# Score blocks transposed in two half-row tiles per pair of heads, in a two-layer attention kernel on one Trainium2 core

## The reference

```python
x = x + L0_attn(layernorm(x))   # 16 heads of 8; logits = q k^T / sqrt(8) - alpha[h] |i - j|
x = x + tanh(((layernorm(x) @ weight) @ aux1) @ aux2 + bias)
x = x + L1_attn(layernorm(x))   # low-rank k and v; scores = (q k^T / sqrt(128)) * exp(-0.01 |i - j|)
x = x + L1_ffn(layernorm(x))    # +-1 weights 256x512, 512x512, 512x128; relu(..) * 2 between them
```

## Time and profile before

| | |
|---|---|
| median of three runs | 350.02 us |
| span of the profiled execution | 348.8 us |
| PE, PEld busy | 330.2 us, 244.0 us |
| DVE, ACT, POOL busy | 275.9, 271.7, 261.3 us |
| item of layer 0, steady state | 17.3 to 18.1 us |
| item of layer 1, steady state | 21.3 us |

### The profile page before, as it was taken

The page is one execution under the profiler, slowest core; times in us unless marked ns, Lnnn a source line. Parts: engine busy times, 40 slices in busy tenths (PEclk is TensorE's granted clock), DMA queues, the critical chain, the costliest instruction groups (busy, mean ns, idle before and its releaser), DMA issues.

```text
span 348.8 us, 11196 instructions
## 1 busy us (share of the span) xinstructions
PE 330.2 (95%) x3550; PEld 244.0 (70%) x3550; DVE 275.9 (79%) x1367; ACT 271.7 (78%) x586; POOL 261.3 (75%) x655
## 2 busy tenths in 40 slices
PE   6599979999999999999999999999999999999986
PEld 4276757777776777777666767777787777778675
DVE  6877778898988998989988888768777677668246
ACT  3576874877776777777878889989898898888943
POOL 7368665676767666767969899898998988898430
PEclk9969998999999999999999999999999999999999
DMA  5202532223233323232332223224132331111001
GB/s 141 69 1 70 161 118 77 97 78 111 84 105 92 95 85 103 78 110 83 105 96 93 80 88 105 74 76 127 36 108 63 89 115 41 43 34 48 2 17 30
DMA packets 42390, 28.14 MB, mean 81 GB/s; under 512 B 9111, under 2 KB 38494, under 8 KB 42334
## 3 DMA queue, kind: packets, MB, share of 16 engines
q1 hardware_dynamic: 41768, 27.18, 26.4%
q10 hardware_dynamic: 566, 0.26, 0.3%
HBM read 14.09 MB, written 13.09 MB: 78 GB/s over the span
## 4 chain that ended last, share of the span: by engine, by line
PE 74%; DVE 9%; DMA 5%; issue 4%; ACT 3%; POOL 2%; SPq 1%; POOLq 0%; DVEq 0%; ACTq 0%
PE bank L551 20%; PE bank L566 14%; PE bank L548 8%; PE bank L592 7%; PE bank L526 5%; PE bank L540 5%; PE bank L613 4%; PE bank L605 3%; DVE scored L854 3%; DMA den_rows<-dden 3%; PE bank L574 2%; PE bank L658 1%; DMA dacc<-acc_sb 1%; PE bank L758 1%; POOL scored L1332 1%
## 5 line engine op out<-in xcount | busy, mean ns | idle before, releaser
L1093 ACT ACTIVATE probs<-bank 128x512 f32<-128x512 f32 x256 | 147.9, 599 | 47.6 <-PE bank L551 31.7
L854 DVE CUSTOM_DVE_ANT_0 scored<-bank,decay 128x256 f32<-128x256 f32 x256 | 93.1, 417 | 28.4 <-PE bank L526 28.2
L551 PE MATMUL bank<-ident,scored 128*128 128x128 f32 x736 | 108.6, 279 | 2.2 <-ACT probs L1093 1.4
L1332 POOL TENSOR_SCALAR scored<-scored,negbias 128x256 f32<-128x256 f32 x224 | 105.5, 487 | 3.1
L854 DVE CUSTOM_DVE_ANT_0 scored<-bank,adist 128x256 f32<-128x256 f32 x256 | 93.1, 417 | 11.0 <-PE bank L526 7.8
L551 PEld LDWEIGHTS bank<-ident,scored 128*128 128x128 f32 x736 | 81.8, 142 | 27.1 <-issue 19.4
L566 PE MATMUL bank<-probs,vpad 128*32 128x256 f32 x1024 | 69.2, 388 | 0.0
L1323 POOL TENSOR_SCALAR negbias<-mx 128x2 f32<-128x2 f32 x144 | 32.8, 237 | 32.0 <-DVE mx L854 31.1
L548 PE MATMUL bank<-ident,scored 128*128 128x128 f32 x288 | 44.4, 278 | 0.0
L566 PEld LDWEIGHTS bank<-probs,vpad 128*32 128x32 f32 x1024 | 26.9, 109 | 24.9 <-ACT probs L1093 7.2
L854 DVE DVE_READ_ACCUMULATOR2_ANT mx<- 128x1 f32 x512 | 42.1, 82 | 0.0
(11 more groups left out here) (196 smaller groups left out, 442.7 us busy)
## 6 DMA issues: line engine op xcount, KB each, us to landing
dqk<-parts SPq DMA_DIRECT2D x120, 64.0 KB, 2.0
stack<-dqk SPq DMA_DIRECT2D x30, 256.0 KB, 2.8
dacc<-acc_sb SPq DMA_DIRECT2D x15, 256.0 KB, 2.2
att_rows<-dacc SPq DMA_DIRECT2D x15, 128.0 KB, 2.6
den_rows<-dden SPq DMA_DIRECT2D x15, 128.0 KB, 2.5
out_dram<-outb SPq DMA_DIRECT2D x7, 128.0 KB, 1.8
x_sb<-in_L_attn_x_dram SPq DMA_DIRECT2D x1, 640.0 KB, 4.7
den_in<-acc_sb SPq DMA_DIRECT2D x30, 8.0 KB
```

The costliest lines, as they stand in the source:

```text
L551: mm = pe.transpose(dst, src, ident[:, :])
L854: red = dve.tensor_tensor_reduce(scored[:, r, t, :], bank[c % QUAD][:, t * T:(t + 1) * T], tab[:, (1 - t) * P:(1 - t) * P + T], 1.0, NEG_B ...
L1093: act.activation(probs[:, c % RING, :, :], turn_bank(c)[:, :].rearrange("p (a c) -> p a c", a=2), ACT.Exp).then_inc(probs_ready, 1)
L1332: sh = pool.tensor_scalar(scored[:, r, t, :], scored[:, r, t, :], negbias[:, 2 * r + t:2 * r + t + 1], 1.0, ALU.add, ALU.mult)
```

## The change

- Heads are turned in pairs. `pe_turn` takes heads 2n and 2n + 1 together. It splits the 128 query rows into two halves of 64. The upper half uses rows 0 to 63 of the array, the lower half rows 64 to 127, each with its own bank. A transpose of 128 x 128 becomes two of 64 rows: the loaded operand is 64 x 128, the streamed one (the identity) has 64 columns. A pair has 16 such transposes, 8 per tile, where it had 8 of full size.
- The two banks of a pair hold each a half of the rows of both heads. `act_exp` reads them one after the other, and the next pair may start only when the banks it takes are read. Both heads and both halves are released by one semaphore at the end of the turn. The banks are 4 and 5, but in layer 0 pair 6 of 8 takes 4 and 6, so pair 7, which takes 5 and 4, waits only for the first exponential of pair 6.
- P is now a property of a pair. `SHIFT` gives 8 of 16 heads to P in layer 0 (7 before) and 6 of 16 in layer 1 (2 before). A P pair has 8 extra products, 4 per tile, of 64 rows and 128 columns. A heads: 3 and 2 (1 and 3 before); G: 4 and 5 (5 and 9 before); D: 1 and 3 (3 and 2 before).
- The heads of D, A and G are written as maximum minus score, and the exponential takes the scale -1. This drops the 144 `negbias` instructions on POOL: the shift reads `mx` itself.
- The product with v stands one slot later (`PV_LAG` 10), banks 6 and 7 change places, all slots are set anew, and the loads of the ±1 weights are issued over items 1 to 3 and not all in item 0.

```diff
+SCORE_AT = 1
+TURNS = (((4, 5), (4, 5), (4, 5), (4, 5), (4, 5), (5, 4), (4, 6), (5, 4)),
+         ((4, 5), (5, 4), (4, 5), (4, 5), (5, 4), (5, 4), (5, 4), (4, 5)))
...
-SHIFT = ("PPGP" "DGGD" "GDPP" "PPGA", "GGGD" "GGAP" "PGDG" "AGAG")
+SHIFT = ("PPAD" "PPPP" "GGPP" "GAGA", "GDDG" "PPGG" "PPDG" "PPAA")
...
-    def pe_turn(pe, c):
-
...
-        need(pe, probs_ready, c + 1 - len(TURN_BANKS))
-        out, r = turn_bank(c), c % RING
-        for t in range(QT if kind == "P" else 0):
-            pe.matmul(out[:, :].rearrange("p (k t q) -> p t k q", k=QT, t=QT)[:, t, :, :],
-                      negmax[:, 2 * r + t:2 * r + t + 1].to_broadcast([P, P]),
-                      ident16[:, :].unsqueeze(1).to_broadcast([P, QT, P]), start=(t == 0), stop=False,
-                      skip_group_check=True)
-        for k in range(QT):
-            for t in range(QT):
-                src, dst = scored[:, r, t, k * P:(k + 1) * P], out[:, k * T + t * P:k * T + (t + 1) * P]
-                if kind == "P":
-                    mm = pe.matmul(dst, src, ident[:, :], start=False, stop=True, is_transpose=True,
-                                   skip_group_check=True)
-                else:
-                    mm = pe.transpose(dst, src, ident[:, :])
+    def pe_turn(pe, n):
+
+
+        pair = (2 * n, 2 * n + 1)
+        banks = turn_banks(n)
+        if pair_is_p(n):
+            pe.wait_ge(shift_p, shifts_p(n + 1))
+        else:
+            for c in pair:
+                kind = shift_of(c)
+                pe.wait_ge({"D": shift_d, "A": shift_a, "G": shift_g}[kind], shifts(kind, c + 1))
+        for b in banks:
+            bank_free(pe, b)
+        halves = [(bank[b], HALF_ROWS * h, slice(HALF_ROWS * h, HALF_ROWS * h + HALF_ROWS))
+                  for h, b in enumerate(banks)]
+
+        for e, t in [(e, t) for e in range(2) for t in range(QT)] if pair_is_p(n) else ():
+            col = 2 * ((2 * n + e) % RING) + t
+            for out, row, rows in halves:
+                pe.matmul(out[:, e * T:e * T + T].rearrange("p (k t q) -> p t k q", k=QT, t=QT)[:, t, :, :],
+                          negmax[rows, col:col + 1].to_broadcast([HALF_ROWS, P]),
+                          ident16[rows, rows].unsqueeze(1).to_broadcast([HALF_ROWS, QT, HALF_ROWS]),
+                          start=(e == 0 and t == 0), stop=False, skip_group_check=True, tile_position=(row, 0))
+        for e, c in enumerate(pair):
+            for k in range(QT):
+                for t in range(QT):
+                    col = e * T + k * P + t * HALF_ROWS
+                    for out, row, rows in halves:
+                        mm = pe.matmul(out[:, col:col + HALF_ROWS], scored[rows, c % RING, t, k * P:(k + 1) * P],
+                                       ident[rows, rows], start=not pair_is_p(n), stop=True, is_transpose=True,
+                                       skip_group_check=True, tile_position=(row, 0))
         mm.then_inc(turned, 1)
+        for h, b in enumerate(banks):
+            last_reader[b] = (probs_ready, 2 * n + h + 1)
...
-    def act_exp(act, c):
-
-        act.wait_ge(turned, c + 1)
-        if c % 4 == 0:
-            need(act, pv_done, c // 4 - 1)
-        act.activation(probs[:, c % RING, :, :], turn_bank(c)[:, :].rearrange("p (a c) -> p a c", a=2),
-                       ACT.Exp).then_inc(probs_ready, 1)
+    def act_exp(act, n):
+
+        act.wait_ge(turned, n + 1)
+        if n % 2 == 0:
+            need(act, pv_done, n // 2 + 1 - RING // 4)
+        r = 2 * n % RING
+        out = probs[:, r:r + 2, :, :].rearrange("p c k (t h q) -> p h (c k t) q", t=QT, h=2)
+        for h, b in enumerate(turn_banks(n)):
+            act.activation(out[:, h, :, :], bank[b][:, :].rearrange("p (a q) -> p a q", q=HALF_ROWS), ACT.Exp,
+                           scale=1.0 if pair_is_p(n) else -1.0).then_inc(probs_ready, 1)
 
     def act_shift(act, c):
 
         in_order("A", c)
 
         r = c % RING
-        act.wait_ge(shift_b, shifts("AG", c + 1))
+        act.wait_ge(max_ready, c + 1)
         for t in range(QT):
             sh = act.activation(scored[:, r, t, :], scored[:, r, t, :], ACT.Identity,
-                                bias=negbias[:, 2 * r + t:2 * r + t + 1])
+                                bias=mx[:, 2 * r + t:2 * r + t + 1], scale=-1.0)
         sh.then_inc(shift_a, 1)
 
     def act_qk(act, n):
...
+    def pool_negmax(pool, n):
+
+        r = 2 * n % RING
+        pool.wait_ge(max_ready, 2 * n + 2)
+        need(pool, turned, n + 1 - RING // 2)
+        pool.tensor_scalar(negmax[:, 2 * r:2 * r + 4], mx[:, 2 * r:2 * r + 4], -1.0, None, ALU.mult).then_inc(shift_p, 1)
+
+    def pool_subtract(pool, c):
+
+        in_order("G", c)
 
         r = c % RING
         pool.wait_ge(max_ready, c + 1)
-        out, done = (negmax, shift_p) if shift_of(c) == "P" else (negbias, shift_b)
-        pool.tensor_scalar(out[:, 2 * r:2 * r + 2], mx[:, 2 * r:2 * r + 2], -1.0, None, ALU.mult).then_inc(done, 1)
-
-    def pool_subtract(pool, c):
-
-        in_order("G", c)
-
-        r = c % RING
-        pool.wait_ge(shift_b, shifts("AG", c + 1))
-        for t in range(QT):
-            sh = pool.tensor_scalar(scored[:, r, t, :], scored[:, r, t, :], negbias[:, 2 * r + t:2 * r + t + 1], 1.0,
-                                    ALU.add, ALU.mult)
+        for t in range(QT):
+            sh = pool.tensor_scalar(scored[:, r, t, :], scored[:, r, t, :], -1.0, mx[:, 2 * r + t:2 * r + t + 1],
+                                    ALU.mult, ALU.add)
         sh.then_inc(shift_g, 1)
 
```

More of the change, by code:

```diff
@@ L116, in shifts, with pair_is_p, shifts_p, turn_banks @@
     return sum(shift_of(k) in kind for k in range(c))
+def pair_is_p(n):
+    assert (shift_of(2 * n) == "P") == (shift_of(2 * n + 1) == "P")
+    return shift_of(2 * n) == "P"
+def shifts_p(pairs):
+    return sum(pair_is_p(n) for n in range(pairs))
+def turn_banks(n):
+    return TURNS[2 * n // (H * B)][n % (H // 2)]
 def layer_of(item):
@@ L132, in has1, with slot, due0, due1 @@
     return has(item) and layer_of(item) == 1
-def at(step, i):
-    if i == 0 and step in FIRST:
+def slot(step, m, lag):
+    if m + lag == 0 and step in FIRST:
         return FIRST[step]
-    return SLOTS[step][has1(i)]
-def at_item(step, m):
-    return SLOTS[step][has1(m)]
+    return SLOTS[step][layer_of(m)]
 def due(step, i, s, lag):
-    return [m for m in (i - lag - 1, i - lag) if has(m) and SLOTS[step][layer_of(m)] == s + H * (i - lag - m)]
-SHIFT_LAG = ("3322212123212121", "1211122323112212")
+    return [m for m in (i - lag - 1, i - lag, i - lag + 1) if has(m) and slot(step, m, lag) == s + H * (i - lag - m)]
+def due0(step, i, s, lag):
+    return [m for m in due(step, i, s, lag) if layer_of(m) == 0]
+def due1(step, i, s, lag):
+    return [m for m in due(step, i, s, lag) if layer_of(m) == 1]
+SHIFT_LAG = ("1321233222322121", "2331332113112211")
 def shift_slot(c):
@@ L958, in dve_iteration @@
             for t in range(QT):
-                if s == at(f"stats{t}", i) and has(n):
-                    dve_ln_stats(dve, n, [t])
-            if s == at("mean", i) and has(n):
-                dve_ln_mean(dve, n)
-            if s == at("hi", i) and has(i + 2):
-                dve_hi(dve, i + 2)
+                for m in due(f"stats{t}", i, s, -3):
+                    if m > 2:
+                        dve_ln_stats(dve, m, [t])
+            for m in due("mean", i, s, -3):
+                if m > 2:
+                    dve_ln_mean(dve, m)
+            for m in due("hi", i, s, -2):
+                if m > 1:
+                    dve_hi(dve, m)
             for step in range(2):
-                if s == at(("rden", "att")[step], i) and has(i - 1):
-                    dve_attention(dve, i - 1, step)
+                for m in due(("rden", "att")[step], i, s, 1):
+                    if m < LAST:
+                        dve_attention(dve, m, step)
             if i == 1 and s == 15:
@@ L971, in dve_iteration @@
                 dve.tensor_copy(bf16[64:65, :], bf_last[64:65, :]).then_inc(bf_ready, 1)
-            if s == at("out_out", i) and has1(i - 3):
-                dve_out(dve, i - 3)
+            for m in due1("out_out", i, s, 3):
+                dve_out(dve, m)
             for m in due("proj_out", i, s, 1):
@@ L976, in dve_iteration @@
             for t in range(QT):
-                if s == at_item(f"f_stats{t}", i - 2) and has(i - 2):
-                    dve_f_stats(dve, i - 2, [t])
-            if s == at_item("f_mean", i - 2) and has(i - 2):
-                dve_f_mean(dve, i - 2)
+                for m in due(f"f_stats{t}", i, s, 2):
+                    dve_f_stats(dve, m, [t])
+            for m in due("f_mean", i, s, 2):
+                dve_f_mean(dve, m)
             if i == 0:
```

260 lines of the change are left out of this document (129 added, 131 removed), and 9 rows, old and new, of tables (FIRST, SLOTS).

## The result

The changed kernel takes 367.44 us (median of four runs, 367.04 to 368.8), the kernel before 350.17 in the same runs: a ratio of 1.052, 95% interval 1.0472 to 1.0569. It is 5% slower. Every ratio here is taken from the runs in the faster of the machine's two states, so it need not equal the quotient of the two medians. I had forecast 347 us and a range that ended at 362.

A forecast was written before the change was run, and what follows sets the result against it. PE was taken to set the pace nearly everywhere; its 33 us saved are nearly all given back to waits. Items 2 to 7 +0.8, 8 to 10 -3, 11 to 14 -0.5, start and end -0.5: 347 us, range 337 to 362.

The forecast's parts named there:

- The loop: Turn and exponentials of a pair take turns on two banks; PE would wait 20 to 30 us for exponentials.
- the floor of the interval: From one pair's exponentials to the next: 1.09 + 0.14 + turn + 0.04, sum 1.91 us; 2.09 for a P pair.
- The half step: One step of a row tile in a turn on PE: 0.056 us, bounds 0.05 and 0.109; 0.45 a pair.
- the term "-55": PE's turns: 8 half steps a pair, 0.45 against 0.88 us, over 128 pairs: -55 us.
- My rival of a longer step: Half step on PE over 0.056 us; at 0.075, +19, 366 us; chance 0.22 together with tiles running one after the other.
- The rule of the Trainium skill quoted in the prediction: A PE load takes its columns divided by 1.2 GHz, whatever the rows: 0.107 us a step, so halves gain nothing.
- The interval before pair 0: In layer-0 items, ACT's vpad, a shift, acc_sb and two exponentials take 2.65 us in all: +0.55.
- My third rival: New waits in ACT's list: shifts of A heads wait for DVE's maximum; +6 to 8 us, 354; chance 0.15.
- "I change nothing": Where the clock is below full, in the first two items, the forecast changed no time.
- a sign of error: A clock below full in steady items, since PE is less dense, would show the forecast wrong.
- the credit of 3 us: Items 8 to 10: -3 us from 56.2, for POOL's fewer heads to shift and no `negbias`.
- "17.35 repeats from item to item": Layer-0 item time before, used as argument against the unexplained 0.45 to 0.7 us an item vanishing.

The follow-up runs named there:

- Kernel 3: Changed kernel with each exponential taking only half its columns, the rest of `probs` constant, so part of the result is left out: 347.85 us (0.9941).
- kernel 5: Changed kernel with one table number changed: in layer 0 ACT copies the accumulator in slot 6, not slot 4: 359.15 us (1.0286).
- kernel 8: Changed kernel with fillers, 8 products without use, ahead of the bank waits in slots 7 and 9 of items 1 to 8: 362.59 us (1.039).
- kernel 6: Changed kernel with whole transposes released head by head, and the layer-0 accumulator copy in slot 6, not 4: 370.69 us (1.062).
- kernel 17: kernel 5 with DVE's reciprocal of the denominators in layer 1 in slot 11, not 9: 365.0 us (1.0406).

## Why the prediction was wrong

**The loop: right in kind, a little short.** The 23.7 + 8.2 us that PE waits for exponentials (20 to 30 forecast), POOL's 194, PE's 309 and layer-1 items of 21.5 are near what I named; items of 17.2 in layer 0 are not: with the clock full they take 18.2 to 19.0. In the chain from 140.47 above the floor of the interval is 1.09 + 0.14 + 0.73 + 0.02 = 1.98 us, not 1.91, since the turn takes 0.73 from its first product to its last end and not 0.67. Kernel 3 shows that the time hangs on the exponentials.

**The half step: too small.** A pair's turn takes 0.50 in the chain, not 0.45 (the rows at 138.41 above), so a step is 0.062 and not 0.056. With 128 pairs that is 6.4 us of PE's work, the term "-55" being -49. My rival of a longer step put +6 at this value and is right in sign, but it explains a third of the miss at most. That its likeliest price, 366 us at a step of 0.075, is close to the measured time is chance: the step is not 0.075. The limit shows in kernel 5: its cleanest layer-0 items (17.1 and 17.5) take little of it. The rule of the Trainium skill quoted in the prediction ("TensorE: Matmul & The Clock Gate", "LDWEIGHTS (loading the stationary operand)") would have made the turn, by an estimate, 8 x 0.107 = 0.86 us; the chain has 0.50, and the measurement decides.

**The interval before pair 0: the step that failed.** I gave it ACT's work (vpad, a shift, acc_sb: +0.55) as if the copy could run at once. The diff moves the value product it waits for from slot 5 to slot 6 and leaves the copy in slot 4. I listed `PV_LAG` as a change and never asked what is queued behind the instruction that waits for it. Kernel 5 puts the price at 8.3 us, clock included. The profiled span misses the forecast by 20.3 us, and in kernel 5 it is 6.7 shorter; of the 13.6 left, 6.4 lie in items 8 to 10, 5.2 in start and end, 1.6 in items 2 to 7. My third rival, new waits inside ACT's list, named another instruction: the shifts wait 0.2 us in all for DVE's maxima, where it had 6 to 8.

**The clock: "I change nothing", wrong.** I had a clock below full as a sign of error but gave it no price. The fillers price it: 4.9 us of the total, and 3.1 and 2.9 us in items 2 to 7 and 8 to 10. Items 2 to 7 so come apart: 114.4 in the changed kernel, 111.3 with the clock held (kernel 8), 107.8 with the copy moved (kernel 5), against a forecast of 106.2.

**Items 8 to 10: the credit of 3 us, wrong.** It stood for POOL's relief. The relief came (POOL is busy 32.1 us there, 50.1 before) and the time did not follow: even with clock and copy mended these items take 59.6, 3.4 over the kernel before. The loss came with the tables and not with the halves, since kernel 6, with whole transposes and a full clock, takes 61.0 there. In items 8 and 9 DVE waits for the denominators (1.0 us in front of two reciprocals) and for the projection (1.2 us), 0.0 and 0.1 before; but the wait of 0.8 us that it had before for their second transfer is gone. In layer 1 the copy had gone from slot 4 to 6 and the reciprocal from 10 to 9; kernel 17 shows that the wait only moves on. DVE also waits 6.2 us for score products there, 3.4 before. What holds these items, and items 3 and 5 of layer 0, stays open. Items 4 and 5 of the kernel before took 18.1 and 17.9 us too, which my "17.35 repeats from item to item" passed over.

**The shape of the change.** That halves and tables are two changes I had not separated. Whole transposes in the new tables 372, halves in the old ones 387, both together 367, neither 350: halves cost 37 us in an order written for single heads, and the order written for pairs takes back 20.

No version that computes the whole result beat the kernel before. The best of the pairs, kernel 5, is 2.9% slower. Not tried was a second pair of banks for the turns, so that PE could turn one pair while ACT reads the other: with two banks, each of which holds a half of both heads, releasing head by head would have PE write a bank that ACT is still reading.

## What to carry to other kernels

When a step moves to a later slot, look up who waits for it and what stands behind that waiter in its own list; here one number cost 8 us. Work saved on the busiest engine is only a gain up to the next loop, so write down the loop's floor with every link in it, and count a shared release of two buffers as the loss of double buffering (39.5 us here). Where the busiest engine starts to wait, price the clock as well: in three items of this kernel, stretches of 3.4 to 6.8 us at half speed followed waits of 1 to 2 us.

## What was not expected of the hardware

- TensorE's clock fell to half in the steady state behind a short lull, not only at the start: PE busy 2.1 to 2.4 of 4 us, then 3.4 or 6.8 us at 1.2 GHz. Products without use in that lull (PE busy 3.2 to 4.0 of 4 us in the same places of kernel 8) kept it at 2.4 GHz and saved 4.9 us. A lull need not bring a fall: 1.28 of 4 us in item 7 of the changed kernel did not.
- PE's list for item 0 met different falls of the clock in different kernels: item 0 had clock 0.71 and took 25.5 us in the changed kernel, 0.93 and 23.6 in kernel 8, whose fillers begin only in item 1. Two profiles can differ by some 2 us for that reason alone.
- Two row tiles of 64 run side by side at 0.062 us per pair of transposes, load of 128 float32 columns included. The streamed 64 columns alone should take 0.056, an estimate from the rows of the kernel before, so little of the load is left outside the stream.
